# Cross-attention scores from one stacked hi/lo tile per head, halves added afterwards, values three slots behind

## The reference, cut to what matters

```python
q = x @ Wq
kv = context @ Wkv
k, v = jnp.split(kv, 2, axis=-1)
q, k, v = (heads(q), heads(k), heads(v))
sim = jnp.einsum('bhid,bhjd->bhij', q, k) * SCALE
sim = jnp.where(mask[:, None, None, :], sim, max_neg)
sim = jnp.clip(sim, -5.0, 5.0)
attn = jax.nn.softmax(sim, axis=-1)
out = jnp.einsum('bhij,bhjd->bhid', attn, v)
```

## Time and profile before

| | us |
|---|---|
| median of 3 runs | 3495.72 (3492.47 to 3499.67) |
| the profiled execution, its own time | 3494.52 |
| its span in the trace | 3492.6 |
| cross attention in it: first scores to the end of its last product on DVE | 112.7 to 2149.5 |

### The profile page before, as it was taken

One profiled execution on the slowest core, in us unless ns is written; L12 is line 12 of the kernel. 1 busy time (PEld: TensorE's weight loads), 2 busy tenths in 40 slices (PEclk: granted clock), 3 DMA queues, 4 the chain that ended last, 5 costly groups with the idle time before them and its releaser, 6 DMA issues. The chain is left out here.

```text
span 3492.6 us, 52773 instructions
## 1 busy us (share of the span) xinstructions
PE 3297.0 (94%) x19140; PEld 2832.4 (81%) x19140; DVE 1810.7 (52%) x2931; ACT 1483.7 (42%) x2755; POOL 1631.5 (47%) x1126
## 2 busy tenths in 40 slices
PE   5999999999999999999999997999999888799997
PEld 4888888888888888888888886867777665678897
DVE  4454554554555555555555455675665645532213
ACT  3455555555555555555555453243443415321000
POOL 4354554554455555555455454131531417246573
PEclk9999999999999999999999998999999999899998
DMA  5211111110111111111111112200000120124221
GB/s 193 73 45 38 46 34 37 46 46 25 46 46 36 35 46 45 38 34 45 38 44 36 37 52 78 73 27 19 9 15 1 53 63 1 42 65 130 85 86 36
DMA packets 117796, 170.05 MB, mean 49 GB/s; under 512 B 12192, under 2 KB 89248, under 8 KB 109344
## 3 DMA queue, kind: packets, MB, share of 16 engines
q1 hardware_dynamic: 114720, 158.17, 14.3%
q0 software_dynamic: 2816, 8.46, 0.7%
HBM read 143.46 MB, written 23.13 MB: 48 GB/s over the span
## 5 line engine op out<-in xcount | busy, mean ns | idle before, releaser
L460 POOL TENSOR_TENSOR es<-es,e 128x512 f32<-128x512 f32 x480 | 620.6, 1293 | 960.9 <-ACT e L530 960.9
L526 ACT ACTIVATE e_hl<-sc 128x512 fp32r<-128x512 f32 x512 | 323.9, 633 | 739.8 <-DVE sc L600 738.6
L558 DVE TENSOR_TENSOR k_lo<-ps_p,k_hi 128x512 fp32r<-128x512 f32 x256 | 175.9, 687 | 439.4 <-ACT k_hi L492 439.4
L558 DVE TENSOR_TENSOR v_hl<-ps_p,v_hl 128x512 fp32r<-128x512 f32 x256 | 177.2, 692 | 426.6 <-ACT v_hl L492 425.6
L600 DVE TENSOR_SCALAR sc<-ps_s,topi 128x512 f32<-128x512 f32 x512 | 379.9, 742 | 0.1
L608 DVE TENSOR_TENSOR e_hl<-e,e_hl 128x512 fp32r<-128x512 f32 x512 | 358.6, 700 | 0.6 <-ACT e L530 0.6
L628 PE MATMUL ps_p<-c_hi,wa 128*128 128x512 f32 x1024 | 339.8, 393 | 4.5 <-PEq L115 4.5
L628 PE MATMUL ps_p<-wa,c_hi 128*128 128x512 f32 x1024 | 337.7, 391 | 0.0
L639 PE MATMUL ps_o<-e_hl,v_hl 128*128 128x256 f32 x2048 | 331.2, 284 | 2.5 <-DVE e_hl L608 2.5
L468 POOL TENSOR_TENSOR c_lo<-raw,c_hi 128x512 fp32r<-128x512 f32 x248 | 321.5, 1296 | 0.0
L530 ACT ACTIVATE e<-sc 128x512 f32<-128x512 f32 x512 | 314.8, 615 | 0.0
(11 more groups left out here) (398 smaller groups left out, 7753.4 us busy)
## 6 DMA issues: line engine op xcount, KB each, us to landing
raw<-in_ctx_t SPq DMA_DIRECT2D x64, 1024.0 KB, 4.9
raw<-in_L_ffn_W_experts SPq DMA_DIRECT2D x64, 256.0 KB, 2.9
raw<-in_L_xattn_Wkv SPq DMA_DIRECT2D x8, 512.0 KB, 4.9
q_hi_scratch<-qa_qh SPq DMA_DIRECT2D x16, 256.0 KB, 2.5
q_lo_scratch<-qa_ql SPq DMA_DIRECT2D x16, 256.0 KB, 3.5
q_hi<-q_hi_scratch SPq DMA_DIRECT2D x32, 128.0 KB, 5.0
q_lo<-q_lo_scratch SPq DMA_DIRECT2D x32, 128.0 KB, 4.6
o_t_scratch<-o_sb SPq DMA_DIRECT2D x32, 128.0 KB, 1.9
```

Of the source, the lines that this page charges most:

```text
L460: g.tensor_tensor(ES[:, GL], ES[:, GL], e, ALU.add).then_inc(summed, 1)
L526: a.activation(E2[:, s % 2, :, 0, :], sc, ACT.Exp, scale=DH ** -0.5).then_inc(exp_hi, 1)
L558: v.tensor_tensor(kv_slice(False, kind, n), ps_view(u, kind), kv_slice(True, kind, n).bitcast(F32), ALU.subtract).then_inc(p_free, 1)
```

## The change

- **Scores.** For each head there is now one stationary tile (`K2`): the head's 64 rows of K_hi above its 64 rows of K_lo. The query tile (`Q2`) holds Q_hi and Q_lo side by side, repeated in both halves of the partitions. One matmul of 256 columns for each head gives two halves, [(K_hi + K_lo)·Q_hi | (K_hi + K_lo)·Q_lo], so 4 matmuls in a slot in place of 6. They fill both banks of `ps_s`, which is no longer double: PE may start slot s only when slot s-1 is clipped.
- **Halves.** ACT copies the right halves of all four heads to SBUF (`RIGHT`), DVE adds them to the left halves in PSUM, waits for its own result (`halves_added`) and clips from there.
- **Key parts.** The rounded keys and their rest are written to a staging tile `KS` (two places, in the memory of `OT`), and four DMAs of 64 rows of 2 KB move each key pair into `K2` (`stack`). ACT waits before it writes a place of `KS` until the DMAs that read it have landed (`k_in`); PE waits for them at slots 0 and 4 of a block; SP waits for `p_free` or `clipped` before it issues them. The zeroing of the query tiles goes away; the queries are read twice, in the same four DMAs.
- **Order.** ACT's exponentials and POOL's sums of slot s-1 are now done in slot s; the values are three slots behind; all group steps are one slot later. The plan of units is turned by one: five units ahead of slot 0 in place of four, the next block's keys in slots 3 to 6, and in the last batch the units end one slot earlier.

The diff, cut to its core:

```diff
-LAG = 2
+LAG = 3
...
-        K_hi = sb("k_hi", [P, HP, BLK], F32R)
-        K_lo = sb("k_lo", [P, HP, BLK], F32R)
+        K2 = sb("k_hl", [P, HP, 2, BLK], F32R)
         V2 = sb("v_hl", [P, KT, 2 * HP, 2 * DH], F32R)
-        Q_hi = sb("q_hi", [P, 2, HP, 2 * P], F32R)
-        Q_lo = sb("q_lo", [P, 2, HP, 2 * P], F32R)
+        Q2 = sb("q_hl", [P, 2, 2 * HP, 2 * P], F32R)
+        RIGHT = sb("right", [P, GRP, P])
+        KS = OT[:].rearrange("p b c t -> p (b c t)").rearrange("p (n e f) -> p n e f", n=2, e=2)
...
-        AHEAD = [(K, 0), (K, 1), (V, 0), (V, 1)]
-        IN_SLOT = [(K, 2, 0), (K, 3, 0), (V, 2, 0), (V, 3, 0), (K, 0, 1), (K, 1, 1), (V, 0, 1), (V, 1, 1)]
+        AHEAD = [(K, 0), (K, 1), (K, 2), (K, 3), (V, 0)]
+        IN_SLOT = [(V, 1, 0), (V, 2, 0), (V, 3, 0), (K, 0, 1), (K, 1, 1), (K, 2, 1), (K, 3, 1), (V, 0, 1)]
         NA = len(AHEAD)
+        NEXT = 3
...
+        def k_landed(i, blk, n):
+
+            return 64 * (2 * (i * SLB + blk) + n // 2 + 1)
...
-                for dst, src in ((Q_hi, q_hi_d), (Q_lo, q_lo_d)):
-                    for hh in range(2):
-                        sp.dma_start(dst[hh * DH:(hh + 1) * DH, hf, :, hh * P:(hh + 1) * P].bitcast(F32),
-                                     src[HP * hf:HP * hf + HP, hh * DH:(hh + 1) * DH, bass.ds(i * P, P)].rearrange("c p t -> p c t")
+                for e, src in enumerate((q_hi_d, q_lo_d)):
+                    for r in range(2):
+                        sp.dma_start(Q2[r * DH:(r + 1) * DH, hf, :, e * P:(e + 1) * P].bitcast(F32),
+                                     src[HP * hf:HP * hf + HP, :, bass.ds(i * P, P)].rearrange("c (h p) t -> p (c h) t", h=2)
                                      ).then_inc(q_in[hf], 16)
-            sp.wait_ge(zeroed, 2)
+
+            def stack(n):
+
+                for hh in range(2):
+                    for e in range(2):
+                        sp.dma_start(K2[e * DH:(e + 1) * DH, n, hh, :].bitcast(F32), KS[hh * DH:(hh + 1) * DH, n % 2, e, :]
+                                     ).then_inc(k_in[n % 2], 16)
             queries(0, 0)
+            for u, (kind, n) in enumerate(AHEAD):
+                if kind == K:
+                    sp.wait_ge(p_free, u + 1)
+                    stack(n)
             load(0, 2)
             load(0, 3)
             queries(0, 1)
...
+                    if s % BS == 0 and (s or not first):
+                        sp.wait_ge(clipped, S)
+                        stack(2)
+                        stack(3)
+                    if s % BS in (KT, KT + 1) and has_kv(s - 1, last):
+                        sp.wait_ge(p_free, unit_at(i, s - 1) + 1)
+                        stack(s % BS - KT)
...
-            for Q in (Q_hi, Q_lo):
-                g.memset(Q[:].bitcast(F32), 0.0).then_inc(zeroed, 1)
...
-                    sums(i, s, first)
+                    if s or not first:
+                        sums(i, s - 1, first)
...
+        halves = ps_s[:].rearrange("p b (j e q) -> p (b j) e q", j=2, e=2)
 
         def kv_slice(hi, kind, n):
             if kind == K:
-                return (K_hi if hi else K_lo)[:, n, :]
+                return KS[:, n % 2, 0 if hi else 1, :].bitcast(F32R)
...
+            def evac_hi(u, par, kind, n, stacked):
                 a.wait_ge(proj_done, u + 1)
+                if kind == K and stacked is not None:
+                    a.wait_ge(k_in[n % 2], stacked)
                 a.copy(kv_slice(True, kind, n), ps_view(par, kind)).then_inc(kv_hi, 1)
 
             for u, (kind, n) in enumerate(AHEAD):
-                evac_hi(u, u, kind, n)
+                evac_hi(u, u, kind, n, k_landed(0, 0, n - 2) if n >= 2 else None)
...
+            def exps(i, s, first):
+
+                S = i * SL + s
+                a.wait_ge(clipped, S + 1)
+                early = first and s < 2
+                if not early:
+                    a.wait_ge(pv_done, S - 1)
+                sc = SC[:, s % 2].rearrange("p (j q) -> p j q", j=GRP)
+                a.activation(E2[:, s % 2, :, 0, :], sc, ACT.Exp, scale=DH ** -0.5).then_inc(exp_hi, 1)
+                if not early:
+                    a.wait_ge(e_lo, S - 1)
+                    a.wait_ge(summed, S - 1)
+                a.activation(E[:, s % 2], SC[:, s % 2], ACT.Exp, scale=DH ** -0.5).then_inc(expd, 1)
+
             def body(i, first, last):
                 for s in range(SL):
                     S = i * SL + s
                     if s and has_kv(s - 1, last) or s == 0 and not first:
-                        evac_hi(unit_at(i, s - 1), unit_at(0, s - 1), *unit_of((s - 1) % SL)[:2])
-                    a.wait_ge(clipped, S + 1)
-                    if not (first and s < 2):
-                        a.wait_ge(pv_done, S - 1)
-                    sc = SC[:, s % 2].rearrange("p (j q) -> p j q", j=GRP)
-                    a.activation(E2[:, s % 2, :, 0, :], sc, ACT.Exp, scale=DH ** -0.5).then_inc(exp_hi, 1)
-                    if not (first and s < 2):
-                        a.wait_ge(e_lo, S - 1)
-                        a.wait_ge(summed, S - 1)
-                    a.activation(E[:, s % 2], SC[:, s % 2], ACT.Exp, scale=DH ** -0.5).then_inc(expd, 1)
+                        kind, n = unit_of((s - 1) % SL)[:2]
+                        evac_hi(unit_at(i, s - 1), unit_at(0, s - 1), kind, n, k_landed(i, (s - 1) // BS + n // 2, (n + 2) % HP))
+                    a.wait_ge(scored, S + 1)
+                    a.copy(RIGHT[:], halves[:, :, 1, :]).then_inc(right_out, 1)
+                    if s or not first:
+                        exps(i, s - 1, first)
...
-                    v.wait_ge(scored, S + 1)
+                    v.wait_ge(right_out, S + 1)
+                    v.tensor_tensor(halves[:, :, 0, :], halves[:, :, 0, :], RIGHT[:], ALU.add).then_inc(halves_added, 1)
                     if not (first and s < 2):
                         v.wait_ge(expd, S - 1)
-                    v.tensor_scalar(SC[:, s % 2], ps_s[:, s % 2], topi[:, kt16:kt16 + 1], -RAW_CLIP, ALU.min, ALU.max).then_inc(clipped, 1)
+                    v.wait_ge(halves_added, S + 1)
+                    v.tensor_scalar(SC[:, s % 2].rearrange("p (j q) -> p j q", j=GRP), halves[:, :, 0, :], topi[:, kt16:kt16 + 1], -RAW_CLIP,
+                                    ALU.min, ALU.max).then_inc(clipped, 1)
...
-                        t.wait_ge(clipped, S - 1)
-                    for pr in range(2):
-                        c = 2 * GL + pr
-                        for n, (k_, q_) in enumerate(((K_lo, Q_hi), (K_hi, Q_lo), (K_hi, Q_hi))):
-                            mm = t.matmul(ps_s[:, s % 2, pr * 256:(pr + 1) * 256], k_[:, c, kt * P:(kt + 1) * P],
-                                          q_[:, hf, c, :], start=n == 0, stop=n == 2)
+                    if kt == 0:
+                        for n in range(2):
+                            t.wait_ge(k_in[n], k_landed(i, s // BS, 2 * GL + n))
+                    if s or not first:
+                        t.wait_ge(clipped, S)
+                    for j in range(GRP):
+                        mm = t.matmul(ps_s[:, j // 2, (j % 2) * 256:(j % 2 + 1) * 256], K2[:, 2 * GL + j // 2, j % 2, kt * P:(kt + 1) * P],
+                                      Q2[:, hf, GRP * GL + j, :], start=True, stop=True)
...
-                        if s % BS == KT and not (first and s < BS):
+                        if s % BS == NEXT and not (first and s < BS):
...
-            total(B, -1)
+            for n in (-2, -1):
+                total(B, n)
```

More of the change, by code:

```diff
@@ L343, in has_kv @@
         def has_kv(s, last):
-            return not (last and s >= SL - BS + KT)
+            return not (last and s >= SL - BS + NEXT)
         def has_split(s, last):
@@ L363, in over_batches @@
             body(B - 1, False, True)
-        TAIL = range(SL, SL + 7)
+        TAIL = range(SL, SL + 8)
         WO_AT = {50: 0, 53: 1, 56: 2, 59: 3}
@@ L416, in body @@
                         sp.wait_ge(o_out, 16 * 4 * 2)
+                        for n in range(2):
+                            sp.wait_ge(k_in[n], k_landed(B - 1, SLB - 1, 2 + n))
                         for b in range(2):
                             sp.dma_start(OT[:, b], o_t[b].rearrange("c p t -> p c t")).then_inc(ot_in, 16)
-                    for n in after(s, 6):
+                    for n in after(s, 7):
                         if n >= 0 or not first:
@@ L434, in _ @@
             g.wait_ge(zero_set, 1)
-            for Q in (Q_hi, Q_lo):
-                g.memset(Q[:].bitcast(F32), 0.0).then_inc(zeroed, 1)
             def group_steps(i, s, first):
-                for n in after(s % SL, 3):
+                for n in after(s % SL, 4):
                     if n >= 0 or not first:
@@ L442, in group_steps @@
                         g.tensor_tensor(ES_lo[:], ES[:, n % 2], ES_hi[:].bitcast(F32), ALU.subtract).then_inc(es_lo, 1)
-                for n in after(s % SL, 4):
+                for n in after(s % SL, 5):
                     if n >= 0 or not first:
```

(6 more changed lines are left out.)

13 lines of the change are left out of this document (8 added, 5 removed).

## The result

| | before | after |
|---|---|---|
| median of 4 runs, us | 3494.09 (3492.10 to 3499.67) | 3439.98 (3438.08 to 3442.43) |
| profiled execution: its own time, span | 3494.52, 3492.6 | 3442.43, 3440.6 |
| attention stage: first scores to last product's end | 112.7 to 2149.5: 2036.8 | 115.2 to 2092.0: 1976.8 |
| all that follows it, code untouched | 1343.1 | 1348.6 |

The ratio is 0.9844 (95% interval 0.9831 to 0.9856): 54 us faster, where 79 were forecast; inside the range. Look at the last two lines of the table: the stage itself gained 60.0 us. The code behind it took 1341 to 1358 us in the executions of this study, whatever was changed before it, so a single trace is best judged by the stage.

What follows compares the result with a forecast made beforehand. The prediction took PE, which waits for nothing, to bound the kernel. -119.7 + 24 + 1 + 10 + 2.7 + 1 + 2 = -79 us gave a forecast of 3415 us, range 3380 to 3458.

Steps and rivals of the forecast that it cites:

- My own case: The prediction's main case for the whole program: 3400 to 3435 us, chance 0.53.
- chain over its cover: Rival: add costs near 1.38 us, or POOL's context part keeps the ports; 3477 or 3485 us, chance 0.17.
- Matmuls removed: PE's slots: two of 6 score matmuls go, 0.236 us in each of 507 slots, -119.7 us.
- The new chain: Scores to clip in a plain slot: clip done at 2.90, PE waits only after 3.55; cover 0.65 us, cost 0.
- three junctions of 0.08: DVE's path in group steps: if each operation started only on an empty pipe, +7 us in all; not counted.
- DVE's lo part against POOL: Shared port in each slot: DVE's lo part of the exponentials, held by POOL's sum, some 1.5 us long; cost 0.
- Group steps: Steady part: DVE's reciprocal starts late, scores 0.78 us late 31 times, +24 us; output copies and additions +1.
- Batch boundaries: Seven batch boundaries: DVE's loop idle and held small copy make scores 1.2 to 1.8 us late, +10 us.
- Key parts by DMA: Key transfers into the stacked tile: 1.9 to 3 us to land with 4.8 available, cost 0.
- Ends: Start and end of the stage: one more unit +2.7, first stack +1, last slots +2 us.
- no queue on DVE: Rival: POOL's sum early enough, or frees DVE sooner, so the reciprocal fits; -108 us, 3387 us, chance 0.18.
- the DMAs were never late: Rival, slower: key DMAs land late at ACT's third key unit copy, up to +183 us, 3598; chance 0.09.

Runs made afterwards that it cites:

- e1: Kernel before with only the K_lo times Q_hi product left out, so 4 score matmuls a slot in place of 6: 3387.20 us, ratio 0.9695 to before.
- e10: Changed kernel with one more DVE instruction of 128x512, its result unused, ahead of the add in each slot: 3501.52 us, ratio 1.0004 to the kernel before.
- e4: Changed kernel with POOL's running sum waiting for DVE's lo part of the same slot, not the exponential: 3424.11 us, ratio 0.9806 to the kernel before.
- e2: Changed kernel with the eight key-part DMAs of each block's slot 0 moved to slot 1: 3439.67 us, ratio 0.9842 to the kernel before.
- e11: Changed kernel with the 1 MB load alone moved from a block's first slot to its third: 3429.80 us, ratio 0.9801 to the kernel before.
- e9: Changed kernel with one more DVE instruction of 128x256, its result unused, ahead of the add in each slot: 3457.41 us, ratio 0.9882 to the kernel before.
- e5: Changed kernel with the 1 MB load moved to a block's third slot and key parts 2 and 3 to its second: 3420.46 us, ratio 0.9788 to before.

## Why the prediction was right, and where its sum was not

The mechanism is right in its main terms, but that the time falls inside the range is partly luck. My own case was 3400 to 3435, and 3440 lies outside it; the range reaches that far only because it takes in the rival *chain over its cover*, which did not come true. What filled the gap is a cost that no rival named.

- **Matmuls removed, -119.7**: right. 2048 score matmuls, and plain slots of 3.70 here and in e1. From 3.94 that is 0.240 and not 0.236 a slot, -121.7.
- **The new chain, 0**: right, with the add at 0.690 as taken from the nearest row. The clip ends at 2.97, not 2.90: it starts 0.80 after the add does, where I had 0.74. Cover 0.53 in place of 0.65, still no cost (e10). The +7 us that the prediction worked out for three junctions of 0.08 did not come: DVE's next operation again starts 0.61 after one of 0.69 (599.02, 599.63).
- **DVE's lo part against POOL**: right. Forecast near 1.5 us, measured 1.322 in the mean, 1.39 in a plain slot; the order is the forecast one: DVE gets its turn between two operations of POOL. `c_lo` (L492) pays for it, 1.724 in the mean against 1.30 in the earlier trace rows. The Trainium skill (SBUF — State Buffer, § SBUF: two separate sides) has the port held for a whole instruction; the trace agrees, and e4 shows that keeping the two apart takes the lo part to 0.683.
- **Group steps, +25**: mechanism right, size too large: 0.53 each where I had 0.78, by the count of 31 16.4 (in the timeline 25 stand by themselves, and five fall under the stalls at the jumps). Behind the group's end POOL's operation is the first of a new sum, with 1.04 us instead of 1.29, so that the reciprocal starts at 0.25 in the slot and not at 0.57. The output copies, +1, cost nothing: their slot is 4.17 (1236.57 to 1240.74), the total's own 0.47 over a plain one. But the multiplication, called hidden, is not hidden in the second group of a half, whose slots also split context: it makes its slot 3.97 (1248.60 to 1252.57) where the first group's is 3.78 (1232.79 to 1236.57), and the next 0.08 longer, 15 times, 4 us.
- **Batch boundaries, +10 for seven: the step that failed.** It took the 1.15 us wait of the earlier trace rows as a fixed cost of the jump and counted it once. Two boundaries, the first and the last, cost next to nothing, as no jump back lies there; the other five cost 7.8 each, 39 in all. Left out were three things: the wait before `topi` was 2.4 and not 1.15 (why it doubled is open); a second wait of 3.2 to 4.2, before the fourth instruction; and 2.3 us for a slot at half clock, after an idle stretch of over 5 us.
- **Key parts by DMA, 0**: right. Landing 2.9 in the median (2.2 to 7.4), issue 0.60 each where I had 0.41, and only two waits of ACT, 4.3 us, at the start. What I had not seen is that the time of a transfer matters at the jump; there it is the load above all (e2, e11).
- **Ends, +5.7**: start +2.5 (115.2 - 112.7) where I had 3.7; this decides nothing, as first scores came between 107.6 and 116.3 in the kernels built on after, with the same code ahead of them; end +4.7 against +2: from slot 59 to the last product 29.05 (2062.96 to 2092.01) against 24.3 of the earlier trace rows. The windows show the clock there, which I left out (columns as above), and PE's timeline one of the last slots:

```profile
112.00:2062.00 1950.00, 1913.59 (x10259) 1648.42 (x10258) 1749.56 (x2155) 1287.56 (x2428) 1141.31 (x817) 0.99 0.46 114
2062.00:2092.00 30.00, 15.12 (x65) 12.72 (x64) 20.58 (x27) 15.14 (x29) 17.63 (x12) 0.58 0.09 22
```

```profile
2072.55 1.22 PE L723 MATMUL ps_s<-q_hl,k_hl 128*128 128x256 f32 x4 [1.41 <-DVE sc L644]
```

PE is busy half of the time there, and the granted clock is 0.58, where in the kernel before it was 0.80 over the 24 us of the earlier trace rows. The last slots' scores take 1.22 instead of 0.64 us, and they lie on the chain.

The sum with what was measured: -121.7 + 16.4 + 4 + 39 + 4.7 = -57.6, against -60.0 in the stage; some 1.5 us of the rest are small delays that the kernel before had at its own jumps. The later start (+2.5) and the code behind the stage (+5.5 in this execution) bring the stage's -60.0 to -52.0, the difference of the two profiled executions; the medians have -54.

Of the rivals, *no queue on DVE* is what e4 makes true by hand; *chain over its cover* would have been so with an add of 1.3; the DMAs were never late. None of the four named a jump. Two of their sums are slightly off: the terms of *no queue on DVE* give +9.7 and not +12 (3 + 1 + 2.7 + 1 + 2), and 0.04 in 507 slots is 20 and not 23.

## What to carry to other kernels

A price read where an engine has time to spare is no price: ask for each wait of a row "issue" what it would be with no slack in front, and whether other transfers go out at that moment. When a change takes an engine from half used to its limit, look first at what happens once per loop iteration, at the jump, and write that loop out where its engine has become tight. Where GpSimd and VectorE read SBUF side by side, order them by a semaphore: here it gave 13 to 16 us, though it made POOL late at the ends of half batches.

## What the runs showed that was not expected

- After a hardware loop's jump back DVE waits 2.2 to 2.8 us before the first instruction in the kernels built on after (1.0 to 1.3 in the kernel before). When a 1 MB load goes out at that moment it waits 2.2 to 4.6 us more before the fourth, but not in e9 and e10, which fetch no code there. Both waits are named in the profile only as `issue`.
- A slot after 5.4 us of idle PE ran at a granted clock of 0.50 and took 6.02 us in place of 3.70; after 2.7 to 2.9 us (e5) it took 5.34 to 5.36 at four of five jumps and 3.78 at the fifth, where the granted clock stayed at 1.00. The idle time is not all that a stall costs.
- Code that follows a changed stage varied by 16 us between executions (1341.4 to 1357.9), more than several of the effects studied here.
